# One-hot, messages and weighted one-hot in three, eight and eight VectorE operations in place of one, two and two

## What is computed

```python
# layer 1: attention over edges (8 heads of 16)
z = (h @ W).reshape(N, 8, 16)
e = leaky_relu(el[src] + er[dst]);  a = exp(e - emax[dst])
agg = segment_sum(z[src] * a[:, :, None], dst);  out = agg / segment_sum(a, dst) + bias
# layer 2: messages from the source's features and an edge's own data
s, v = scalar part and vector part of h, each times a weight
w0, w1, w2, w3 = split(silu(silu(edge_feats @ A1 + b1) @ A2 + b2) @ A3, 4)
out_s0 = ss * y_s * w0;  out_s3 = einsum(vs, y_v) / R3 * w3
out_v1 = ss * y_v * w1;  out_v2 = vs * y_s * w2
message = segment_sum(concatenate(out_s0, out_s3, out_v1, out_v2), dst) / 10
```

## Time and profile before

| | |
|---|---|
| Median of 3 runs | 4207.77 us (4206.33 to 4208.55) |
| Span of the profiled execution | 5708.3 us |
| Time of the profiled execution beside its span | not recorded |
| TensorE matmuls, busy | 3872.9 us (68%) |
| GpSimd, busy | 3121.2 us (55%) |
| VectorE, busy | 1850.8 us (32%) |
| ScalarE, busy | 547.9 us (10%) |
| Mean granted TensorE clock, share of full | 0.643 |

### The profile page before, as it was taken

One profiled execution on the slowest core, in us unless ns is written; L12 is line 12 of the kernel. 1 busy time (PEld: TensorE's weight loads), 2 busy tenths in 40 slices (PEclk: granted clock), 3 DMA queues, 4 the chain that ended last, 5 costly groups with the idle time before them and its releaser, 6 DMA issues.

```text
span 5708.3 us, 68375 instructions
## 1 busy us (share of the span) xinstructions
PE 3872.9 (68%) x18070; PEld 2962.4 (52%) x18071; DVE 1850.8 (32%) x4774; ACT 547.9 (10%) x1093; POOL 3121.2 (55%) x3153
## 2 busy tenths in 40 slices
PE   3566666766666666666657776776777776667767
PEld 2455555555555555555545555555555555555545
DVE  6122222222222222222234443433333434333334
ACT  1000000000000000000021111111111111111111
POOL 4555555555555555555535555555555555555554
PEclk8555555555555555555567777777777877777777
DMA  3111111111111111111111111111111111111111
GB/s 75 40 40 40 40 40 41 41 42 40 41 40 41 40 41 39 41 40 40 40 43 41 42 45 41 44 45 41 42 43 43 44 44 41 44 40 43 42 41 34
DMA packets 259081, 239.77 MB, mean 42 GB/s; under 512 B 179890, under 2 KB 205596, under 8 KB 259068
## 3 DMA queue, kind: packets, MB, share of 16 engines
q0 software_dynamic: 100352, 212.14, 15.2%
q1 hardware_dynamic: 158572, 26.68, 2.6%
q10 hardware_dynamic: 144, 0.80, 0.0%
HBM read 229.11 MB, written 10.23 MB: 42 GB/s over the span
## 4 chain that ended last, share of the span: by engine, by line
another core or an unknown queue 43%; PE 22%; issue 17%; DVE 11%; DVEq 4%; ACT 2%; DMA 0%; ACTq 0%; SPq 0%
PE pair L1085 5%; PE pair L1050 5%; DVE share L809 4%; PE pair L1044 3%; PE pair L1083 3%; PE pair L1040 2%; DVEq L768 2%; ACT share L502 1%; PE pair L1062 1%; PE pair L1004 1%; PE pair L987 1%; DVE share L743 1%; DVE share L800 1%; DVE share L799 1%
## 5 line engine op out<-in xcount | busy, mean ns | idle before, releaser
L401 POOL DMA_INDIRECT rows<-z_tab,idx x1568 | 1531.6, 977 | 1290.3 <-DVEq L813 748.9
L401 POOL DMA_INDIRECT rows<-up_tab,idx x1568 | 1549.4, 988 | 1208.6 <-DVEq L896 718.1
L1004 PE MATMUL pair<-share 128*128 128x48 f32 x3136 | 1000.7, 416 | 122.6 <-issue 122.3
L1004 PEld LDWEIGHTS pair<-share 128*128 128x128 f32 x3136 | 808.4, 317 | 279.4 <-issue 273.3
L1085 PE MATMUL pair<-share 128*128 128x144 f32 x3136 | 859.4, 359 | 129.8 <-issue 129.3
L1083 PEld LDWEIGHTS pair<-share 128*128 128x128 f32 x3136 | 587.2, 219 | 443.2 <-issue 342.9
L1050 PE MATMUL pair<-a_bd,share 128*128 128x256 f32 x1576 | 465.9, 448 | 394.1 <-ACT share L504 371.1
L877 DVE TENSOR_TENSOR share<-share,y_sb 128x768 f32<-128x768 f32 x392 | 375.6, 958 | 977.1 <-remote 662.1
L1083 PE MATMUL pair<-share 128*128 128x48 f32 x3136 | 585.7, 269 | 140.0 <-issue 121.2
L1085 PEld LDWEIGHTS pair<-share 128*128 128x128 f32 x3136 | 561.3, 221 | 128.6 <-issue 128.0
L987 PE MATMUL pair<-er_win,share 96*128 96x32 f32 x1576 | 377.2, 404 | 333.0 <-issue 268.4
(11 more groups left out here) (138 smaller groups left out, 2085.3 us busy)
## 6 DMA issues: line engine op xcount, KB each, us to landing
rows<-z_tab,idx POOLq DMA_INDIRECT x1568
rows<-up_tab,idx POOLq DMA_INDIRECT x1568
idx<-in_src SPq DMA_DIRECT2D x396, 4.0 KB
er_win<-er_tab SPq DMA_DIRECT2D x396, 3.0 KB
ef_sb<-in_edge_f SPq DMA_DIRECT2D x198, 32.0 KB
z_tab<-rows SPq DMA_DIRECT2D x7, 476.0 KB, 3.1
y_sb<-in_edge_y SPq DMA_DIRECT2D x198, 16.0 KB
x_sb<-in_x SPq DMA_DIRECT2D x7, 448.0 KB, 6.9
```

The costliest lines, as they stand in the source:

```text
L401: pool.indirect_dma_start(out=rows[:, s, t, 0:width], out_offset=None, in_=table, in_offset=bass.IndirectOffsetOnAxis(ap=indices[:, t:t + ...
L1004: t.matmul(bank[2 + h][:, 0:WIN], msg[:, h, i, :], hot[:, s, i, :], start=(i == 0), stop=(i == T - 1))
```

## The change

The same three results are made by more and smaller operations. In layer 1 the one-hot of a group is made in three operations (three, three and two columns of 48), and the messages column by column, eight of 128 elements in place of two of 512. In layer 2 `wy` is made column by column, eight operations of 192 elements a group in place of two of 768. The semaphores are incremented at the same points: by the last of the three, and by the last of each four. Elements, places and order are the same; the access patterns have one dimension fewer in `msg` and `wy`.

```diff
             def one_hot(s, group):
-                v.tensor_tensor(hot[:, s, :, :],
-                                bc(dst_rel[:, bass.ds(group, 1), :].rearrange("p a t -> p (a t)"), 2, WIN),
-                                bc(iota[:, :], 1, T), ALU.is_equal).then_inc(s_l1["hot"], 1)
+                to = dst_rel[:, bass.ds(group, 1), :].rearrange("p a t -> p (a t)")
+                for ts in (slice(0, 3), slice(3, 6), slice(6, T)):
+                    ins = v.tensor_tensor(hot[:, s, ts, :], bc(to[:, ts], 2, WIN),
+                                          bc(iota[:, :], 1, ts.stop - ts.start), ALU.is_equal)
+                ins.then_inc(s_l1["hot"], 1)
...
                         for hf in range(2):
-                            ts = slice(hf * HT, hf * HT + HT)
-                            ins = v.tensor_tensor(msg[:, h, ts, :].rearrange("p t (h f) -> p t h f", f=PER_HEAD),
-                                                  rows[:, s, ts, 0:HIDDEN].rearrange("p t (h f) -> p t h f", f=PER_HEAD),
-                                                  bc(a_sb[:, h, ts, :], 3, PER_HEAD), ALU.mult).then_inc(s_l1["msg"], 1)
+                            for i in range(hf * HT, hf * HT + HT):
+                                ins = v.tensor_tensor(msg[:, h, i, :].rearrange("p (h f) -> p h f", f=PER_HEAD),
+                                                      rows[:, s, i, 0:HIDDEN].rearrange("p (h f) -> p h f", f=PER_HEAD),
+                                                      bc(a_sb[:, h, i, :], 2, PER_HEAD), ALU.mult)
+                            ins.then_inc(s_l1["msg"], 1)
...
                             dve.wait_ge(s_l2["half_free"], n * (2 * U) + (2 * s + hf + 1))
-                            v.tensor_tensor(wy[:, hf, :, :].rearrange("p t (k w) -> p t k w", k=4),
-                                            bc(eq[:, hf, :, :], 2, 4),
-                                            bc(y_sb[:, s, ts, :], 3, WIN), ALU.mult)
+                            for i in range(HT):
+                                v.tensor_tensor(wy[:, hf, i, :].rearrange("p (k w) -> p k w", k=4),
+                                                bc(eq[:, hf, i, :], 1, 4),
+                                                bc(y_sb[:, s, hf * HT + i, :], 2, WIN), ALU.mult)
```

## The result

On the chip of the times shown before, the changed kernel takes 4213.14 us (median of 12, 4206.36 to 4222.12) and the kernel before 4206.32 us (12 runs, 4201.1 to 4209.9): ratio 1.0018 [1.0009, 1.0026]. Run again beside the kernel before on a second chip it takes 4232.78 us (5 runs) against 4219.19 us (9 runs): ratio 1.0035 [1.0021, 1.0049]. The prediction was 4120 us.

A forecast was written before the change was run, and what follows sets the result against it. Gather issue on GpSimd was taken as the bound. Shorter holds would gain 116 or 127 us by two sums, 70 to 81 scaled to the budget; 88 was taken, giving 4120 us, range 4070 to 4175.

The forecast's parts named there:

- Gather issue bounds, and VectorE's extra work is hidden: Both layers: gathers take 9.98 us per group; about 170 us more VectorE time costs the span below 1 us.
- The 0.12 us rule: A gather starting during a VectorE instruction with two SBUF inputs is let go about 0.12 us before its recorded end.
- So GpSimd gets in between two instructions.: Between back-to-back VectorE operations a held gather goes when the first ends; read from the gather at 130.77, losing 0.33 us.
- The rival of the held train: Gathers wait for all eight or four short instructions: +0.97 us a group, +190 us, 4398 us; chance 0.06.
- The phase of the first layer: First layer, gathers keeping step: the gather at +4.99 us hits the second L809 and loses 0.52 us.
- After: about 0.05: Keeping step, after the split: the three holds per group become about 0.05, 0.02 and 0.17 us, 47 us in all.
- The second layer: Weighted one-hot, L877: the gathers at +4.99 and +8.84 us lose 0.11 and 0.26 us a group before the change.
- The budget of 111 us: Holds that the measured 4207.8 us leave room for after gathers, start, gap, tail and set-up: 111 us, give or take 50.
- both ways: Two sums of holds: gathers starting at random, 184 to 68 us, gain 116; keeping step, 174 to 47 us, gain 127.
- GpSimd's waits for VectorE will again fill the profiled span.: Profile after the change: the long slot waits, 1467.0 us before, return, so the span itself says little.
- No change: Rival: unprofiled runs meet few holds, perhaps 75 us now and as many after; 4200 to 4216 us; chance 0.07.
- VectorE or TensorE as the bound: Rival: all 170 us of added VectorE time would show, 4378 us; chance 0.03.

The follow-up runs named there:

- the fastest one: One-hot in three, messages in two with the exponentials read from PSUM, weighted one-hot in eight, against the kernel before: 4133.78 us, ratio 0.9801.

## Why the prediction was wrong, step by step

- **Gather issue bounds, and VectorE's extra work is hidden.** Right: 92% of the chain, and ten kernels whose time follows the holds while VectorE's busy time goes from 1889 (messages in 4 alone) to 2064 us. The trains grew by 0.14 (L745), 0.42 (L811) and 2 x 0.20 us (L881) a group, 0.96 where the sum had 0.86.
- **The 0.12 us rule and which operations hold.** Right, also that one input in PSUM holds nothing: none of 199 gathers that began in line 812's trains was over 0.01 us too long. The Trainium skill's rule (SBUF — State Buffer, Who interferes with whom) holds for the kinds of operations; that GpSimd is kept out for the one instruction that it meets, and no longer, holds for the one-hot's pieces and the weighted one-hot's of 128 and 192, and not for the messages of 128.
- **"So GpSimd gets in between two instructions."** This is the step that failed. It rested on the one row at 130.77, between two operations of 512. In the messages' train of 128, 71 of 136 gathers held in the fifth piece and 30 of 31 in the sixth waited for the train's end, and the holds in the messages came to 83 us. 57 of these are waiting beyond the first opening, of the 95 us between the forecast (88 gained) and the result (7 lost). The prediction's own sign of being wrong, gathers that last beyond the piece they start in, came true. The rival of the held train had the mechanism, but put it in both layers and in every case: +190 us. In messages of 256, which let gathers go, the same change takes 4158.79 us against 4219.08: 60 us gained, so the openings alone don't give the 88 either.
- **The phase of the first layer.** Wrong as well; the rest of the gap is mostly here. The forecast had one hold of 0.52 at +4.99, in the second L809, 102 us in all, and about 10 after. In the kernel before there were 61 us, mostly in L743, and that hold carried the next gather past the messages. The term that was mis-sized is the landing: 2.96 us after the last gather's start, read at the layer's first group (no other one of that trace is under 9 us, as VectorE is late at all of them); in the layer without the long waits the median is 2.68. With 2.68 the prediction's own steps put L743 at +3.61, under the gather at +3.74, and the next gather just behind the messages. "After: about 0.05" needed both that the gathers go at piece ends and that the phase be kept; with the messages in four, 43 us of holds stay. In that kernel the first layer's term, 92 us before scaling, gave 17 (60.6 - 43.2), while the second's 36 gave 46 (65.2 - 19.6).
- **The second layer.** Right: 0.37 us a group, 73 us, was 65; after, 0.19 and 37, was 20 to 29 in the five kernels with the weighted one-hot in eight.
- **The budget of 111 us**, to which both ways were scaled: 109 to 112 on the chip that it was worked out for, 126 in the traces from the others. It took one gather of 6 us out as set-up's; with the other two it is 8.4.
- **"GpSimd's waits for VectorE will again fill the profiled span."** They did not: the profiled execution after has none of the long waits.
- **The rivals.** No change was given 0.07, on a knife edge of landing times. The time did come out near it (4213 in 4200 to 4216), by luck and another way: a loss in one layer against a gain in the other. VectorE or TensorE as the bound is out: together they make 6% of the chain.

**Left open:** why the messages of 128 hold a gather to the train's end. It needs their second SBUF input, and it isn't the size alone (weighted one-hot in 128) nor the messages alone (256 elements go). It goes by the place in the train: in the three traces of messages in eight, 82 of 84 held gathers that began in the first four pieces went at the end of their own, 121 of 294 in the fifth, and 3 of 184 that began later with an opening still ahead. What differs there, the semaphore that the fourth piece increments, the rows that the gathers themselves write or the exponential's pattern, wasn't tried apart.

## What to carry to other kernels

When a queue of short GpSimd instructions is the bound, price each VectorE operation by what it does to the phase of the **next** one as well as by its own hold: a delay removed at one place can be paid at the next, and parts that are worth -39, +20 and +48 us alone can't be added: they make +29, and together they measured +7 and +14. Where a VectorE operation holds GpSimd, moving one of its inputs to PSUM is surer than cutting it up: it doesn't depend on the phase, and costs VectorE no operation (here it cost ScalarE a second exponential per group, in its idle time). And a rule taken from one row ("it gets in between two instructions") should be tried at the size that the change uses before a sum rests on it.

## What the runs showed of the hardware

- A gather issued while VectorE works on two SBUF inputs goes 0.12 us before the recorded end of its own piece in the weighted one-hot's trains of 128 and 192, the messages' of 256 and the one-hot's of 144 elements, and in those of 96 but for the last piece but one (63 of 64 ran on). In the messages' train of 128 it went there in 65 and 56 cases of those begun in the fifth piece, and only at the end of the train in 71 and 102, at 1.57 us of 1.70.
- Between holds the gathers keep their pace to 0.3 us in 2000: the stretch from the first to the last start of a layer, less its holds, is 1956.6 to 1956.9 us in both layers of all eleven traces without the long waits (2146.0 - 91.3 - 97.9 in the changed kernel's first layer; 2059.2 - 90.8 - 11.7 in the fastest one's).
- On two chips ScalarE and VectorE meet waits of about 12 us (median of VectorE's over 8 us: 11.7 and 9.9), ended by nothing named, that make every execution 1.5 ms longer; there the one-hot's split alone cost 3.4% and 3.6%. The place of these waits changed with the program.
